# Head attention: the loop over pairs of images becomes straight-line code on all five engines

## The reference, cut to what matters

```python
router_in = hidden_states.mean(axis=1)
logits = router_in @ Wr + br
_, top_idx = jax.lax.top_k(logits, K)            # K = 6 of 12 heads
...
q = proj(Wq, bq) * m                             # (image, head, 1024 tokens, 32)
k = proj(Wk, bk) * m
v = proj(Wv, bv) * m
scores = jnp.einsum('bhqd,bhkd->bhqk', q, k) / jnp.sqrt(jnp.float32(D))
probs = jax.nn.softmax(scores, axis=-1)
ctx = jnp.einsum('bhqk,bhkd->bhqd', probs, v)
...
x = ctx @ Wo + bo + hidden_states
mu = x.mean(axis=-1, keepdims=True)
var = ((x - mu) ** 2).mean(axis=-1, keepdims=True)
return (x - mu) / jnp.sqrt(var + EPS) * ln_g + ln_b
```

## Time and profile before

| what | value |
|---|---|
| median of 3 runs | 3693.16 us |
| lowest and highest | 3691.4 and 3697.67 us |
| the profiled execution, its own time | 3696.41 us |
| its span, first to last instruction | 3694.4 us |
| mean granted TensorE clock | 0.953 |
| PE, DVE, ACT, POOL busy | 90%, 73%, 61%, 39% of the span |

### The profile page before, as it was taken

One profiled execution on the slowest core, in us unless ns is written; L12 is line 12 of the kernel. 1 busy time (PEld: TensorE's weight loads), 2 busy tenths in 40 slices (PEclk: granted clock), 3 DMA queues, 4 the chain that ended last, 5 costly groups with the idle time before them and its releaser, 6 DMA issues. The chain is left out here.

```text
span 3694.4 us, 65555 instructions
## 1 busy us (share of the span) xinstructions
PE 3335.8 (90%) x18046; PEld 1927.0 (52%) x18046; DVE 2714.7 (73%) x5169; ACT 2257.3 (61%) x5369; POOL 1456.9 (39%) x1544
## 2 busy tenths in 40 slices
PE   7969999999999999947999999968888888888897
PEld 3434444444444444436888888844444444434443
DVE  4468888888888888756888888846677677766765
ACT  3434444444444444355777777746877778777785
POOL 2144444444444444272222222221254454544535
PEclk9979999999999999968999999978999999999997
DMA  9999989889999899541000000011222322232221
GB/s 362 370 356 345 333 333 351 324 328 338 349 340 342 336 343 347 221 171 37 17 17 17 17 17 17 17 64 45 84 74 64 91 72 65 78 87 64 59 66 55
DMA packets 230577, 647.44 MB, mean 175 GB/s; under 512 B 31142, under 2 KB 127942, under 8 KB 229958
## 3 DMA queue, kind: packets, MB, share of 16 engines
q0 software_dynamic: 82944, 453.02, 32.7%
q1 hardware_dynamic: 147398, 191.91, 16.4%
HBM read 520.21 MB, written 79.18 MB: 162 GB/s over the span
## 5 line engine op out<-in xcount | busy, mean ns | idle before, releaser
L697 PE MATMUL b_acc<-b_sampled,b_w 128*128 128x512 f32 x2592 | 1210.8, 594 | 0.0
L632 DVE SCALAR_TENSOR_TENSOR b_mix<-shared,b_weight,b_mix 128x384 f32<-128x384 f32 x864 | 531.8, 621 | 140.6 <-ACT b_mix L655 82.6
L697 PEld LDWEIGHTS b_acc<-b_sampled,b_w 128*128 128x128 f32 x2592 | 449.1, 191 | 347.5 <-issue 347.5
L664 ACT ACTIVATE b_sampled<-b_tps 128x384 f32<-128x384 f32 x576 | 282.7, 491 | 566.5 <-PE b_tps L715 556.6
L1988 DVE TENSOR_REDUCE e_neg_top<-e_next 128x1 f32<-128x1024 f32 x384 | 469.8, 1224 | 211.1 <-PE e_next L2301 171.4
L632 DVE SCALAR_TENSOR_TENSOR b_mix<-b_got,b_weight,b_mix 128x384 f32<-128x384 f32 x864 | 530.8, 619 | 92.6 <-ACT b_mix L655 55.9
L2140 ACT ACTIVATE e_unused<-e_next,e_neg_top 128x1024 bf16<-128x1024 f32 x384 | 430.1, 1120 | 117.1 <-DVE e_neg_top L1988 104.8
L2155 ACT ACTIVATE e_prob<-e_s 128x512 f32<-128x512 f32 x768 | 416.9, 598 | 125.3 <-PE e_s L2313 124.3
L588 POOL DMA_INDIRECT shared<-corner_table,b_index x288 | 294.7, 1023 | 418.7 <-DVE b_mix L632 291.9
L588 POOL DMA_INDIRECT b_got<-corner_table,b_index x288 | 292.6, 1016 | 356.8 <-DVE b_mix L632 282.7
L715 PEld LDWEIGHTS b_tps<-ident,b_mix 128*128 128x128 f32 x1728 | 223.0, 142 | 371.9 <-issue 328.2
(11 more groups left out here) (225 smaller groups left out, 5360.2 us busy)
## 6 DMA issues: line engine op xcount, KB each, us to landing
corner_table<-y SPq DMA_DIRECT2D x32, 1536.0 KB, 14.8
e_stack<-e_high SPq DMA_DIRECT2D x384, 64.0 KB, 2.0
shared<-in_x SPq DMA_DIRECT2D x8, 1536.0 KB, 10.1
c_x<-in_x SPq DMA_DIRECT2D x16, 768.0 KB, 4.4
tokens<-y SPq DMA_DIRECT2D x64, 192.0 KB, 1.9
e_tok<-tokens SPq DMA_DIRECT2D x8, 1536.0 KB, 7.3
e_stack<-e_low SPq DMA_DIRECT2D x192, 64.0 KB, 2.0
shared<-tokens SPq DMA_DIRECT2D x8, 1536.0 KB, 7.2
```

The lines of the kernel that those rows point to most:

```text
L632: ins = nc.vector.scalar_tensor_tensor(dst[:], src[:, q * C:(q + 1) * C], weight[g][:, q, k, i:i + 1], dst[:], ALU.mult, ALU.add)
L664: nc.scalar.activation(sampled[s % 2][:, :, i * P:(i + 1) * P], tps[t % 2][:, 0:C].rearrange("p (o q) -> p o q", q=P), ACT.Copy).then_inc( ...
L697: last = nc.tensor.matmul(acc[g][co][:], w_conv[:, k, ci, co * P:(co + 1) * P], sampled[s % 2][:, ci], start=(k == 0 and ci == 0), stop=(k ...
```

## The change

In `turns`, which PE, DVE, ACT and POOL share, and in SP's own copy of it, the device loop becomes a Python loop that writes out every turn. With it `n` is a Python number in all turns, so all counts of waits and all addresses of images are constants. No arithmetic, tile, DMA or order of work changes. The loops of the other stages stay.

```diff
@@ def turns(eng, turn):
             turn(0, 0, tail=False)
-            with eng.Fori(0, BATCH // 2 - 1) as j:
-                turn(2 * j + 1, 1)
-                turn(2 * j + 2, 0)
+            for n in range(1, LAST):
+                turn(n, n % 2)
             turn(LAST, 1, prep=False)
@@ block.sync
                 turn(0, 0, tail=False)
-                with sp.Fori(0, (BATCH - 4) // 2) as j:
-                    turn(2 * j + 1, 1)
-                    turn(2 * j + 2, 0)
-                turn(LAST - 2, 1)
+                for n in range(1, LAST - 1):
+                    turn(n, n % 2)
                 turn(LAST - 1, 0, load=False)
                 turn(LAST, 1, prep=False, load=False)
```

## The result

The changed kernel takes 3675.4 us (median; 3672.31 to 3679.36). Beside it the kernel before takes 3693.16 us (3691.4 to 3697.67). The ratio is 0.995, with a 95% interval of 0.9939 to 0.9961. That is 17.8 us less, where 17.2 us was forecast (3676.0 us).

A forecast was written before the change was run, and what follows sets the result against it. Pauses at two back edges, with coupled engines and no single engine limiting a turn, were taken as the main cost: 13.2 + 3 (VectorE registers) + 1 (SyncE) = 17.2 us off 3693.2 gives 3676.0 us, range 3668 to 3687.

The forecast's parts named there:

- The back edges, 13.2 us: Head attention's loop: two branches back, at turns 2 to 3 and 4 to 5, cost 13.2 us together; bounds 11.8 to 15.4.
- The step at the end of a turn: VectorE's maximum before a turn's end to its first `e_ctx` after: 13.73 us with a back edge, 7.39 without, 6.34 more.
- The long intervals: Between GpSimd's weight-scaling starts, those containing a back edge: 150.42 and 150.30 us; all should become 142 to 145 us.
- The registers, 3 us on VectorE and 1 us on SP: Head attention's turns: exposed register instructions for counts cost 3 us on VectorE (0 to 9.2) and 1 on SyncE (0 to 2).
- A third of VectorE's places: Of VectorE's 22 waits a turn at 0.07 us, 9.2 us in six turns, a third taken as on the path: 3 us.
- TensorE's and ScalarE's registers, put at nothing: Register instructions on these engines in the turns cost nothing; TensorE's run while earlier matmuls still stream.
- The added code, nothing: Written-out turns in head attention: each is fetched once, the bytes read are no more, and the cost is nothing.
- The engines would have waited anyway: Rival at turn ends: the pause only covers a wait for the residual's image load; 3690 to 3693 us, 6 in 100.
- Slower, straight-line code comes late: Rival at ends of turns 1 to 6: fetches queue behind the image load, 6.6 us each; 3715 us, 4 in 100.
- Half comes back: Rival: turns after a pause profit as SP and GpSimd catch up, leaving 9 us gain; 3684 us, 7 in 100.
- More of the waits counts: Rival: all of VectorE's 9.2 us and SP's 2 us lie on the path; gain 24.4 us, 3669 us, 8 in 100.
- A delay on one of them is soon a delay on all: Inside a turn TensorE, VectorE and ScalarE pass two small buffers around, so no engine alone is the limit.

The follow-up runs named there:

- the kernel with loaded registers: Kernel before, its loop written out, but turns 1 to 5 (SyncE 1 to 4) take counts and addresses from a register loaded from memory: 3680.27 us, ratio 0.9962.
- the moved load: Residual image's 1.5 MB load moved into the next turn's first step: 3685.71 us in the kernel before (ratio 0.998), 3675.69 us in the changed kernel.

## Why the prediction was right

**The back edges, 13.2 us.** Right in kind, and in size within the scatter: 12.1 us by the kernel with loaded registers, or about 11.2 us without the sixth turn's registers; its interval of 4.8 us each way also holds 13.2. The step at the end of a turn is 6.44 us shorter (13.73 to 7.29), where 6.34 was read. The long intervals are gone, and each experiment that keeps a branch on TensorE, VectorE or ScalarE keeps a pause. That the image's load in flight lengthens what the branch waits for is shown by the moved load (6.7 us back from a change that touches no branch, and none without a loop). That it is the code is inferred: a wait at a taken branch, in which the instruction queues q8 and q14 move packets (one and three between 2946.4 and 2952.8 us in the kernel before, by the DMA view), and no such wait in code that doesn't branch.

**The registers, 3 us on VectorE and 1 us on SP.** Together 4.6 to 4.9 us were measured for five turns, by the estimate above 5.5 to 5.9 us for six, so 4 us was somewhat low. A third of VectorE's places was a guess between 0 and 9.2 us; that it came near is luck. So is the agreement of the sums to 0.6 us (17.2 forecast, 17.8 measured): the back edges came out some 2 us lower than their term and the registers some 2 us higher, and both lie within the scatter. TensorE's and ScalarE's registers, put at nothing, show no cost beyond the scatter of a turn (91.64 and 91.06 us in the table, against 91.34 to 91.37). SP's part was seen in the trace (0.24 to 0.07 us) but not priced by itself.

**The added code, nothing.** Right: straight-line code has no pause at any end of a turn, with the DMA engines 0.99 busy at the end of turn 2. At the end of turn 4 the instruction queues moved two packets within 7 us of the load's start (3221.7 us), and no engine stood for them. From 2580 to 3620 us these queues moved 1.03 MB instead of 1.40, so the bytes read are less, as the prediction's count of fetches had it.

**The rivals.** "The engines would have waited anyway" falls: the changed kernel doesn't wait at the place of the pause. "Slower, straight-line code comes late" falls with it. "Half comes back" falls by the total and by the interval in which no back edge lies (142.9 us against 143.8, not more). "More of the waits counts" would have been 3669 us; by the 5.5 to 5.9 us above, about half of that case's 11.2 us came.

**Where the working was incomplete.** "A delay on one of them is soon a delay on all" holds in full for TensorE alone and only in part for ScalarE and VectorE alone, whose long intervals are 2.3 to 5.2 us longer and not 6.6. The kernel with TensorE alone in the loop loses 19 us. Its two branches (6.3 and 7.0 us), or 15.9 us by its two long intervals, don't explain all of it; 2.1 us more lie in turn 0 of the profiled execution. Why TensorE's two back edges alone cost as much as those of all engines together (14.9 us, counted in the same way) is open, and so is most of the 7 us that TensorE alone written out gains.

## What to carry to other kernels

When several engines stand at the same moment with idle time put down to "issue", look for a compare-and-branch that takes microseconds: here such a branch waited at each back edge, most likely for the code at the head of a long body. It shows on TensorE's sequencer alone: in the source view of L1586, VectorE's and ScalarE's branches read 40 to 74 ns although these engines stood as well, so look at their timelines too. Write such a loop out on all engines that are coupled, since one left in it brought back 10.6 to 19 of 17.8 us, or, if that isn't possible, keep large loads away from the back edge, which here gave 6.7 of 17.8 us. An experiment on registers must take them from memory; with a value that was known at build time it measured nothing here.

## What the runs showed of the hardware

- A back edge to a long body cost 6.1 and 6.2 us on TensorE's sequencer with 1.5 MB in flight, and 3.4 and 3.7 us without. ScalarE stood for 5.57 and 2.32 us. So a load in flight about doubles the wait. In straight-line code no such wait appeared, even with the DMA engines 0.99 busy.
- The Trainium skill, "Runtime: NRT & Kernel Launch", Instruction fetch mechanics, says that a taken branch out of the held pages must fetch first. The runs agree with it. With any one of three engines alone in the loop the kernel lost 5.3 to 9.5 us per branch by the medians (10.6, 12.6 and 19 us for two).
- A wait count worked out in a register costs VectorE some 0.07 to 0.09 us where it follows an instruction that its sequencer has just waited for (0.23 against 0.14 us behind `e_fin`), and nothing visible on TensorE and ScalarE (91.64 and 91.06 us for the stretch into turn 1, against 91.34 to 91.37 without registers and 93.27 with VectorE's).
- After a pause with TensorE idle for 4.63 us the granted clock was 0.50 (1.2 GHz); after one of 2.19 us the first pair ran in 0.72 us, as at full clock, but over the 4.2 us from there the granted clock was 0.60. A pause half as long so brought the lower clock too, a little later.
